# Attention over positions in the last layer: PE's order staggered, the maxima subtracted by GpSimd, row sums from the value product, the residual moved into the normalisation

## The reference, cut to what matters

```python
def _L3_ffn_ref(hidden_states, ...):
    S, B, H = hidden_states.shape            # 32, 128, 128
    ln1 = _layer_norm(hidden_states, ln1_weight, ln1_bias)
    qkv = jnp.einsum('sbh,oh->sbo', ln1, qkv_weight)
    ...
    scores = jnp.einsum('bgqsd,bgtd->bgqst', qb, kb) * scale
    scores = jnp.where(causal, scores, jnp.finfo(scores.dtype).min)
    attn = jax.nn.softmax(scores, axis=-1)
    ao = jnp.einsum('bgqst,bgtd->bgqsd', attn, vb)
    ...
    proj = jnp.einsum('sbh,oh->sbo', ao, proj_weight)
    h1 = hidden_states + proj
    ln2 = _layer_norm(h1, ln2_weight, ln2_bias)
    ... # routing and experts give moe_out from ln2
    return h1 + moe_out.reshape(S, B, H)

x = x + jnp.tanh(g_ffn[3]) * _L3_ffn_ref(_layernorm(x, axis=-1), ...)
```

## Time and profile before

| | before |
|---|---|
| median of 3 runs | 3308.88 us (3307.4 to 3314.95) |
| profiled execution | 3294.93 us, span 3293.2 us |
| granted TensorE clock, mean | 0.909 of 2.4 GHz |
| PE busy | 2890.1 us (88%) |
| DVE busy | 2162.1 us (66%) |
| ACT busy | 1787.4 us (54%) |
| POOL busy | 1352.1 us (41%) |
| attention over positions, first to last masking of scores | 2818.8 to 2984.6 us |
| first normalised tile of "n3m" | 3013.1 us |

### The profile page before, as it was taken

One profiled execution on the slowest core, in us unless ns is written; L12 is line 12 of the kernel. 1 busy time (PEld: TensorE's weight loads), 2 busy tenths in 40 slices (PEclk: granted clock), 3 DMA queues, 4 the chain that ended last, 5 costly groups with the idle time before them and its releaser, 6 DMA issues. The chain is left out here.

```text
span 3293.2 us, 68941 instructions
## 1 busy us (share of the span) xinstructions
PE 2890.1 (88%) x21504; PEld 2288.4 (69%) x21504; DVE 2162.1 (66%) x8122; ACT 1787.4 (54%) x5161; POOL 1352.1 (41%) x1646
## 2 busy tenths in 40 slices
PE   7999989948697999999999689999999984774998
PEld 5888744417554888888888578888888863564676
DVE  5544447738645555555555299999999996897332
ACT  5777634423223655555555378788888842331332
POOL 2112237737201333333333168778777865211000
PEclk9999979965698999999999899999999965996999
DMA  3000023322300000000000000000000000001000
GB/s 108 6 6 6 4 65 78 64 80 77 109 0 0 1 0 0 0 0 0 0 0 1 5 6 6 6 6 7 6 6 6 6 28 1 10 13 30 0 0 26
DMA packets 53866, 63.52 MB, mean 19 GB/s; under 512 B 5664, under 2 KB 37936, under 8 KB 53168
## 3 DMA queue, kind: packets, MB, share of 16 engines
q1 hardware_dynamic: 53696, 61.73, 6.6%
HBM read 57.19 MB, written 4.39 MB: 19 GB/s over the span
## 5 line engine op out<-in xcount | busy, mean ns | idle before, releaser
L1610 POOL TENSOR_TENSOR l2a_probs<-l2a_probs,l2a_inv 128x1024 f32<-128x1024 f32 x128 | 242.3, 1893 | 475.8 <-DVE l2a_inv L1776 475.8
L1721 ACT ACTIVATE l2a_probs<-l2a_s_ps,l2a_nm 128x256 f32<-128x256 f32 x512 | 237.2, 476 | 225.9 <-DVE l2a_nm L1752 225.9
L2500 DVE MAX8 l3a_top<-l3a_work 128x8 f32<-128x128 f32 x1536 | 313.6, 273 | 0.0
L2344 PEld LDWEIGHTS l3a_l2o_ps<-net_arena 128*128 128x128 f32 x2048 | 267.7, 215 | 65.0 <-issue 37.3
L2344 PE MATMUL l3a_l2o_ps<-net_arena 128*128 128x128 f32 x2048 | 279.4, 302 | 33.1 <-ACT net_l1f_gate L2405 30.5
L2206 POOL TENSOR_SCALAR l3a_above<-l3a_score,l3a_top 128x128 f32<-128x128 f32 x512 | 299.1, 603 | 16.4 <-DVE l3a_work L2502 6.0
L2502 DVE MATCH_REPLACE8 l3a_work<-l3a_top,l3a_work 128x128 f32<-128x128 f32 x1024 | 268.5, 272 | 0.0
L2331 PE MATMUL l3a_l2h_ps<-net_cols,net_arena 128*128 (+1 forms) x1024 | 248.4, 386 | 11.0 <-PEq L1817 7.6
L2442 ACT ACTIVATE net_arena<-l3a_l2h_ps,net_l2f_b 128x256 f32<-128x256 f32 x512 | 212.0, 486 | 38.6 <-PE l3a_l2h_ps L2331 35.7
L2331 PEld LDWEIGHTS l3a_l2h_ps<-net_cols,net_arena 128*128 128x128 f32 x1024 | 184.8, 191 | 60.4 <-issue 28.9
L685 ACT ACTIVATE l0a_probs<-l0a_score_ps,l0a_nm 128x128 f32<-128x128 f32 x512 | 180.0, 383 | 73.4 <-DVE l0a_nm L734 73.4
(11 more groups left out here) (523 smaller groups left out, 7222.0 us busy)
## 6 DMA issues: line engine op xcount, KB each, us to landing
l0f_code<-code_rows SPq DMA_DIRECT2D x32, 512.0 KB, 10.5
l1a_shift<-neg_top SPq DMA_DIRECT2D x16, 512.0 KB, 3.5
net_x<-x SPq DMA_DIRECT2D x4, 512.0 KB, 6.4
l0a_c_in<-ctxT SPq DMA_DIRECT2D x32, 64.0 KB, 1.8
net_arena<-L_w1T SPq DMA_DIRECT2D x1, 2048.0 KB
net_arena<-L_w2T SPq DMA_DIRECT2D x1, 2048.0 KB
l3a_k_in<-ctxT SPq DMA_DIRECT2D x32, 64.0 KB, 1.8
l3a_v_raw<-ctx SPq DMA_DIRECT2D x32, 64.0 KB, 1.9
```

What stands on the lines that cost most here:

```text
L1610: pool.tensor_tensor(p[:, :, :], p[:, :, :], per_row(inv[c % 2][a][:, :, :].rearrange("p i o -> p (i o)"), KV), ALU.mult).then_inc(scaled, 1)
L1721: act.activation(probs[c % 2][a][:, 2 * i + odd, :], s_ps[a][odd][:, i * KV:(i + 1) * KV], ACT.Exp, bias=nm[c % 2][a][:, i, odd:odd + 1], ...
L2344: ins = pe.matmul(o2_ps[:, at:at + D], hidden[2 * x + n][:, i, j * P:(j + 1) * P], w2[:, expert(u, 2 * x + n), i, :], start=(i == 0), stop ...
L2500: ins = dve.max(t[:, step // 2, h, :], src)
```

## The change

- `schedule` takes a hook `between`, unrolls iterations -2 to 3, loops 7 times over four, and ends with the remaining steps unrolled, so that each step runs for exactly 32 rounds.
- PE's steps are split and put in another order; q's copy goes from DVE to ACT; DVE starts a round with `soften`.
- The subtraction of the maxima goes to POOL (`shift`).
- v tiles become 4 groups of 36 columns: 32 of v and 4 of ones for the own heads (filled once by POOL). The value product then gives the row sums in its last 4 columns; the row sums by DVE and their wait are gone.
- y moves from `out_ps` to the first bank of the scores, with waits both ways.
- After the loop SP reads back the first 112 positions of the result, after the last stores the other 16, into `k.attended`. `l3_block_residual` is gone; `normalise` "n3m" does the additions, four before the statistics of each half, and the updates of `k.x` after the last normalised tile.

```diff
                 for half in halves:
+                    if attended is not None:
+                        for g in range(half.start // G4, half.stop // G4):
+                            tiles = slice(g * G4, g * G4 + G4)
+                            dve.tensor_tensor(k.rows[:, tiles, :], k.rows[:, tiles, :], attended[:, tiles, :], ALU.add
+                                              ).then_inc(joined, 1)
+                        dve.wait_ge(joined, half.stop // G4)
...
+                if attended is not None:
+                    for g in range(NG):
+                        tiles = slice(g * G4, g * G4 + G4)
+                        dve.scalar_tensor_tensor(out=k.x[:, tiles, :], in0=k.rows[:, tiles, :], scalar=k.tg[:, 7:8],
+                                                 in1=k.x[:, tiles, :], op0=ALU.mult, op1=ALU.add).then_inc(x_joined, 1)
...
-        v = [s.sb(f"v{i}", [P, PJ, P]) for i in range(4)]
+        WV = R * HD + R
+        v = [s.sb(f"v{i}", [P, PJ, GK, WV]) for i in range(4)]
...
-        o_ps, aoT_ps, y_ps = (out_ps[:, i * P:(i + 1) * P] for i in range(3))
+        o_ps = out_ps[:, 0:GK * WV].rearrange("p (g w) -> p g w", g=GK)
+        aoT_ps = out_ps[:, GK * WV:GK * WV + P]
+        y_ps = s_ps[:, 0, P:2 * P]
...
-        def schedule(eng, steps):
-            for c in range(-1, 2):
+        def schedule(eng, steps, between=None):
+            for c in range(-2, BODY):
                 for step, behind in steps:
                     if c - behind >= 0:
                         step(0, c - behind)
-            with eng.Fori(0, NN // BODY) as q:
-                for c in range(2, 2 + BODY):
+            with eng.Fori(0, NN // BODY - 1) as q:
+                for c in range(BODY, 2 * BODY):
                     for step, behind in steps:
                         step(q, c - behind)
+            if between is not None:
+                between()
+            for c in range(BODY, 2 * BODY):
+                for step, behind in steps:
+                    if c - behind < BODY:
+                        step(NN // BODY - 1, c - behind)
...
-                schedule(sp, [(store, 2)])
-                for i in two:
-                    sp.wait_ge(y_stored[i], 16 * NN // 2)
+                def stored(n):
+                    for i in two:
+                        sp.wait_ge(y_stored[i], 16 * n // 2)
+                def take_back(first, last):
+                    sp.dma_start(k.attended[first * PJ:last * PJ, :, :],
+                                 k.block_out[:, first * PJ:last * PJ, :].rearrange("s t d -> t s d")).then_inc(att_in, 16)
+                def take_most():
+                    stored(NN - BODY)
+                    take_back(0, NN - BODY)
+                schedule(sp, [(store, 2)], take_most)
+                stored(NN)
+                take_back(NN - BODY, NN)
+                sp.wait_ge(att_in, 32)
...
+                for t in v:
+                    pool.tensor_copy(t[:, :, :, R * HD:WV].rearrange("p j g r -> p (j g) r"), per_group(own_head[:, :], PJ * GK)
+                                     ).then_inc(made, 1)
...
+                def shift(q, c):
+                    t = score[c % 2]
+                    wait(pool, maxed, q, 1, c + 1)
+                    pool.tensor_tensor(t[:, :, :], t[:, :, :], per_row(mx[c % 2][:, :], S), ALU.subtract
+                                       ).then_inc(shifted, 1)
+                schedule(pool, [(gather, -2), (shift, 0)])
...
-                    wait(pe, y_ready, q, 1, c)
+                    wait(pe, aoT_ready, q, 1, c)
                     for j in range(PJ):
                         for g in range(GK):
-                            ins = pe.matmul(o_ps[S * j:S * j + S, 32 * g:32 * g + 32], pT[:, g, S * j:S * j + S],
-                                            v[c % 4][:, j, 32 * g:32 * g + 32], start=True, stop=True)
+                            ins = pe.matmul(o_ps[S * j:S * j + S, g, :], pT[:, g, S * j:S * j + S], v[c % 4][:, j, g, :],
+                                            start=True, stop=True)
...
-                def output(q, c):
+                def turn_out(q, c):
                     wait(pe, ao_ready, q, 1, c + 1)
                     pe.transpose(aoT_ps, ao[:, :, :].rearrange("p h d -> p (h d)"), k.ident[:, :]).then_inc(aoT_mm, 1)
+                def output(q, c):
                     wait(pe, aoT_ready, q, 1, c + 1)
+                    wait(pe, y_ready, q, 1, c)
+                    wait(pe, s_out, q, 1, min(c + 3, NN - BODY * q) if isinstance(q, int) else c + 3)
+                    wait_apart(pe, k.waited_pe)
                     pe.matmul(y_ps, aoT[:, :], proj[:, :], start=True, stop=True).then_inc(y_mm, 1)
-                schedule(pe, [(project, -1), (scores, 0), (output, 2), (apply, 1)])
+                schedule(pe, [(scores, 0), (project, -1), (turn_out, 2), (turn_probs, 1), (values, -1), (output, 2), (apply, 1)])
...
-                schedule(act, [(take_out, 2), (take_p, 1), (exps, 0)])
+                def take_q(q, c):
+                    wait(act, k_mm, q, 1, c + 1)
+                    wait(act, s_mm, q, 1, c - 1)
+                    act.activation(qT[c % 2][:, :], q_ps, ACT.Copy).then_inc(q_ready, 1)
+                schedule(act, [(take_q, -1), (take_turned, 2), (take_p, 1), (take_out, 2), (exps, 0)])
...
-                    wait(dve, maxed, q, 1, c + 1)
-                    dve.tensor_tensor(t[:, :, :], t[:, :, :], per_row(mx[c % 2][:, :], S), ALU.subtract
-                                      ).then_inc(shifted, 1)
-                def total(q, c):
-                    wait(dve, exped, q, 1, c + 1)
-                    dve.tensor_reduce(sums[c % 2][:, :], score[c % 2][:, :, :], AX.X, ALU.add).then_inc(summed, 1)
-                    wait(dve, summed, q, 1, c + 1)
-                    dve.reciprocal(inv[c % 2][:, :], sums[c % 2][:, :]).then_inc(inv_ready, 1)
                 def divide(q, c):
                     wait(dve, o_mm, q, 1, c + 1)
+                    dve.reciprocal(inv[:, :, :], o_ps[:, :, R * HD:WV]).then_inc(inv_ready, 1)
                     wait(dve, inv_ready, q, 1, c + 1)
                     wait(dve, aoT_mm, q, 1, c)
-                    dve.tensor_tensor(ao[:, :, :], o_ps.rearrange("p (h d) -> p h d", h=H), per_row(inv[c % 2][:, :], HD),
-                                      ALU.mult).then_inc(ao_ready, 1)
-                schedule(dve, [(take_qk, -1), (take_v, -1), (soften, 0), (total, 1), (divide, 1)])
...
+        k.attended = Space(nc, ctx, "l3").sb("attended", [P, NB, D])
         normalise(nc, k, "n3f", gains=k.l3b_w, twice=True, gain=norms[:, 0:1], shift=norms[:, 1:2], keep_rows=True)
         l3_block_attention(nc, k)
-        l3_block_residual(nc, k)
-        normalise(nc, k, "n3m", gains=k.l3b_w, source="rows", gain=norms[:, 2:3], shift=norms[:, 3:4],
+        normalise(nc, k, "n3m", attended=k.attended, gains=k.l3b_w, source="rows", gain=norms[:, 2:3], shift=norms[:, 3:4],
                   gate_w=k.gates_w[:, 3, :], logits=k.logits)
```

More of the change, by code:

```diff
@@ L245, in normalise @@
 def normalise(nc, k, name, source="x", twice=False, gain=None, shift=None, keep_rows=False,
-              gate_w=None, columns=None, logits=None, fetch=(), after=None, gains=None, arriving=None):
+              gate_w=None, columns=None, logits=None, fetch=(), after=None, gains=None, arriving=None,
+              attended=None):
     tiled = columns is not None
@@ L2543, in l3_block_attention @@
         score = [s.sb(f"score{i}", [P, H, S]) for i in two]
-        mx, sums, inv = ([s.sb(f"{n}{i}", [P, H]) for i in two] for n in ("mx", "sums", "inv"))
+        mx = [s.sb(f"mx{i}", [P, H]) for i in two]
+        inv = s.sb("inv", [P, GK, R])
         pT = s.sb("pT", [P, GK, P])
@@ L2630, in project @@
                     tokens = stage[c % 2][:, :, :].rearrange("p j s -> p (j s)")
-                    wait(pe, staged, q, 2, 2 * c + 2)
+                    wait(pe, staged, q, 2, 2 * c + 1)
                     wait(pe, k_ready, q, 1, c)
@@ L2634, in project, with values @@
                     pe.matmul(k_ps, wk[:, :], tokens, start=True, stop=True).then_inc(k_mm, 1)
+                def values(q, c):
+                    wait(pe, staged, q, 2, 2 * c + 2)
                     wait(pe, v_ready, q, 1, c)
@@ L2645, in scores @@
                     wait(pe, s_out, q, 1, c)
+                    wait(pe, y_ready, q, 1, c - 2)
                     wait_apart(pe, k.waited_pe)
@@ L2712, in take_v @@
                     wait(dve, o_mm, q, 1, c - 3)
-                    dve.tensor_tensor(v[c % 4][:, :, :], v_ps[:, :].rearrange("p (j n) -> p j n", j=PJ), own_cols[:, :, :],
-                                      ALU.mult).then_inc(v_ready, 1)
+                    dve.tensor_tensor(v[c % 4][:, :, :, 0:R * HD].rearrange("p j g n -> p (j g) n"),
+                                      v_ps[:, :].rearrange("p (m n) -> p m n", m=PJ * GK),
```

(30 more changed lines are left out.)

20 lines of the change are left out of this document (11 added, 9 removed).

## The result

| | before | changed |
|---|---|---|
| median, same chip | 3308.14 us (4 runs, 3298.02 to 3314.95) | 3249.14 us (4 runs, 3236.07 to 3262.62) |
| ratio | | 0.9826, 95% interval 0.9803 to 0.9849 |
| profiled execution | 3294.93 us, span 3293.2 | 3236.07 us, span 3234.5 |
| a second comparison, same two kernels | 3309.11 us (9 runs) | 3254.17 us (5 runs), ratio 0.9835, 0.9813 to 0.9857 |

The change is faster by 59.0 us in the first comparison and 54.9 in the second.

What follows compares the result with a forecast made beforehand. DVE, close to full, was taken as the bound, at 5.1 us a round. Steps 6.6+113.1+16+13.5 = 149.2 instead of 195.1, and -2.4 at the start, gave -48.3: 3246.6 profiled, median 3261 us, range 3250 to 3282 (its own 3250 to 3269).

Steps and rivals of the forecast that it cites:

- start, to scores(0): Attention's start: second q, k and values groups go behind the first scores, POOL fills ones; net -2.4 us.
- scores(0) to scores(2): First two attention rounds: they lack work but run partly at the low clock; 6.6 us, an estimate.
- scores(2) to scores(31): The other attention rounds: 29 at 3.9 us each, 113.1 us, with the two wrapped rounds gone.
- scores(31) to the first addition: Attention's tail: last results, their store, the read-back and the block's end; 16 us, far end 19.
- addition to the first normalised tile: Normalisation with the residual inside: two times four additions at 2.54 us, the rest unchanged at 8.44; together 13.5 us.
- All four arrivals: Waits within a round: probabilities, ao, pT and y's copy reach PE in time; slack 0.7, 0.18 (4.60 against 4.78), 0.5, 0.35 us.
- it lands at S31+12.5: Tail: the early read of 112 positions, 1.84 MB at 246 GB/s, lands 12.5 us after the last round's scores start.
- Hold by the power: Normalisation: the second half's additions wait 2.3 us for GpSimd's power; 3263 us, chance 0.06.
- Gaps on PE: Attention rounds: PE idles 0.20 us at two or three more group changes; round 4.4, +14.5, 3276 us; chance 0.20.
- GpSimd in the path: Attention rounds: each GpSimd instruction stretched by 1.1 us; round 4.6, +20, 3281 us; chance 0.10.
- The lag does not help: Attention rounds: value product, divide and transpose of ao stay serial; round near 5.1, +35, 3296 us; chance 0.04.
- Slower: Attention rounds: TensorE falls to 1.2 GHz; round near 6.6, +78, 3339 us; chance 0.03.

Runs made afterwards that it cites:

- new_order: The changed kernel with q's copy, the subtraction of the maxima and the row sums back on DVE, PE's new order kept: 3286.24 us (before beside it 3307.41).
- old_order_y_apart: The changed kernel with PE's order of before and y's result back in the output's bank: 3295.64 us (before beside it 3309.98).
- old_order: The changed kernel with PE's order of before, work moved off DVE and y in the scores' bank kept: 3323.33 us (before beside it 3307.41).
- direct: The changed kernel with each result stored from SBUF straight to its rows of the attended tile, no DRAM trip or read-back: 3246.49 us, ratio 0.9813 to before.
- residual_apart: The changed kernel with read-back, additions and updates of x in their own stage again behind the attention: 3256.99 us (before beside it 3302.11).

## Why the prediction was right, and where it was off

| step | predicted | measured |
|---|---|---|
| start, to scores(0) | -2.4 | -2.7 (40.6 to 37.9 after the first statistics) |
| scores(0) to scores(2) | 6.6 | 6.5 |
| scores(2) to scores(31) | 113.1 (3.9 each) | 106.8 (3.68 each) |
| scores(31) to the first addition | 16 | 19.9 |
| addition to the first normalised tile | 13.5 | 13.5 |
| the change in all | -48.3 | -51.0 |

That the sum came out so near is in part luck: the rounds were forecast 6.3 us too long and the tail 3.9 too short. The forecast of the median, 3261, was 11.9 us too high against the first comparison and 6.8 against the second, and the stage accounts for only 2.7 of that.

**What bounded the kernel: right in the conclusion, incomplete in the reason.** "DVE is close to full" named DVE as the limit. Its 27.36 of 30 us are 4.65 us a round, and new_order ran at 4.70. But the round was 5.10, and the rows that said why were in the prediction: PE idle 0.37 and 0.69 us, both times for ACT, never for DVE. PE's serial chain was the limit, DVE the next one 0.4 us behind it. old_order_y_apart shows it: DVE at 61%, the round unchanged. The forecast didn't suffer, as it worked out the new PE chain in full and took DVE off the path as well.

**The round: 3.68 for 3.9.** Three terms of the sum were too large. The value product: 0.93, in proportion to its columns, measured 0.85, against 0.83 with 32 columns. The Trainium skill, "TensorE: Matmul & The Clock Gate", section "Back-to-back issue gap", states the issue floor that the prediction weighed and didn't take; the trace agrees with it: 0.85 us for 32 instructions is 27 ns each, at 36 columns nearly as at 32. Values took 0.89 for 0.98: a group's distance to the next depends on which group follows, and in old_order, where the scores follow again, it was 0.99 (2873.07 to 2874.06). The transposes took 0.55 for 0.59, which had been read from the busy time of their loads. Sum 3.59 for 3.80. The margin of 0.1 for gaps was right in size: six turns of the loop at 0.4 us, over 29 rounds, are 0.08 a round. But they lie at the loop, and not before the groups.

**The waits.** All four arrivals came as worked out, counted from the start of scores:
- Exponentials end at +3.95 (2891.49 + 0.63 - 2888.17), predicted +4.2, since the subtraction took 1.05 and not 1.27. The nearest row, a 128x512 tensor_tensor on POOL at 1273 ns, had two full inputs; this one has a full one and one of 16 numbers per partition.
- ao ends at 2888.86 and its transpose's load begins at 2889.04: slack 0.18, as predicted. This is the tightest way, and new_order, where DVE is late, waits there.
- pT's copy ends at 2890.49 and the value product's loads begin at 2890.90: slack 0.41, predicted 0.5.
- y's copy ends at 2891.37, the next scores start at 2891.76: slack 0.39, predicted 0.35. In old_order the same bank, met from the other side, cost 0.5 us a round at full clock.

**The tail: 19.9 for 16.** The term "it lands at S31+12.5" was mis-sized: the read of 1.84 MB was issued where predicted, at +4.1, but took 10.4 us. 8.5 were reckoned, at the 246 GB/s of a window with reads alone. The last 256 KB took 4.4 us where 2.84 was taken from the first old read: that one went to 128 partitions, this one goes to 16. Traffic around it is not the reason: from its issue to its landing the windows (in the columns of the earlier trace rows) show 55 GB/s over 4.8 us, which is this read and nothing more. That the 16 partitions are the reason is likely, and no run varies them.

```profile
2936.40:2941.20 4.80, 0.00 (x0) 0.00 (x0) 0.00 (x0) 0.00 (x0) 0.00 (x0) 0.50 0.30 55
```

SP's rows show the rest:

```profile
SPq L2615 <- DMA block_out<-l3b_y: 4.8, 1, 4.8
SPq L2603 <- DMA l_attended<-block_out: 4.1, 1, 4.1
```

SP waited 4.8 us for the last stores and 4.1 for the last read. direct, without either read, gets 6.0 to 6.3 us of the tail back: that is what the trip through DRAM cost. Of the 19.9 us, 8.9 are the last results' own way to y's copy, as forecast.

**The residual: right.** 13.5 as predicted, the updates of x hidden as predicted. Moving it was worth 2.3 to 3.3 us net (residual_apart): it saves 6.4, and 3.8 go again before the first addition.

**The rivals.** *Hold by the power*: refuted, the four additions beside the 3.28 us of power took 2.51 us, those before it 2.50. By the rule in the Trainium skill, "SBUF — State Buffer", section "Who interferes with whom", they would have been held; this trace disagrees, as the earlier trace rows had. The power, for its part, took 3.28 us beside the additions and 2.91 in the kernel before, without them; that fell on no path that matters. *Gaps on PE*: only at the turns of the loop, 0.4 us six times. *GpSimd in the path*: no, 1046 to 1051 ns over 32 rounds, none stretched. *The lag does not help*: refuted, and it helps only beside the lighter DVE. *Slower*: the clock stood at 1.00 from 2810 us to the last round. But its mechanism is real here: in old_order TensorE fell to 0.81 on average in the last rounds, after 30 us (2930 to 2960) in which PE had been busy 21.81, and seven rounds took about 2.0 us more than those at full clock in old_order_y_apart, where PE was busy 39.84 of 50 us and the clock held.

**Open.** The medians differ by 59.0 and 54.9 us, the stage by 51.0 and 50.0. The interval of the first comparison reaches to -50 and that of the second to -47, so they agree. Of the kernel before there is one profile alone, so whether any of the remaining 5 to 8 us is the change's own stays open.

## What to carry to other kernels

An engine busy 91% of a stretch need not be its limit: look for the engine whose idle times, each named, add up with its work to the round, and for the next limit behind it, since two limits close together must both be moved (5.09 and 4.74 alone, 3.65 together). A result that moves to another bank brings that bank's waits along, harmless in one order (slack 0.39 us) and 0.5 us a round in another, before the clock fell. Price a read from DRAM by a row with the same number of partitions and the same traffic around it, and ask first whether the data need to leave SBUF.
